# Out-projections, stores, loads and first products of a half at other places of a written-out order; the fill of a phase's middle score bank given to VectorE

## The reference, cut to what matters

```python
x = L0_attn_x                                  # (8, 1024, 256), float32
x = x + 0.5 * ffn(layernorm(x))                # 8 routed experts (top 2) and a shared one
x = x + attention(layernorm(x))
x = x + 0.5 * ffn(layernorm(x))

def attention(x):                              # x is (b, s, 256); 16 heads of 64
    h = layernorm(x) * ln_scale + ln_bias
    c_q, c_kv = h @ w_down_q.T, h @ w_down_kv.T            # 128 wide each
    q, k, v = c_q @ w_up_q.T, c_kv @ w_up_k.T, c_kv @ w_up_v.T
    q, k = rope(q), rope(k)
    attn = softmax(q @ k.T / 8)                # over 1024 keys
    return (attn @ v) @ w_out.T + x
```

## Time and profile before

| what | value |
|---|---|
| median of 3 runs | 4161.7 us |
| lowest and highest of them | 4150.89 and 4165.04 us |
| the profiled execution's own time | 4144.14 us |
| its span, first to last instruction | 4142.2 us |
| its mean granted TensorE clock | 0.986 |
| attention part, from its first transpose to the next part | 528 to 3630 us of the span |

### The profile page before, as it was taken

One profiled execution on the slowest core, in us unless ns is written; L12 is line 12 of the kernel. 1 busy time (PEld: TensorE's weight loads), 2 busy tenths in 40 slices (PEclk: granted clock), 3 DMA queues, 4 the chain that ended last, 5 costly groups with the idle time before them and its releaser, 6 DMA issues. The chain is left out here.

```text
span 4142.2 us, 65717 instructions
## 1 busy us (share of the span) xinstructions
PE 3935.1 (95%) x24908; PEld 2209.9 (53%) x24908; DVE 2790.7 (67%) x3709; ACT 2630.8 (64%) x3276; POOL 2955.7 (71%) x1634
## 2 busy tenths in 40 slices
PE   7999979999999999999999999999999999989999
PEld 6888834444444444444444444444444444468888
DVE  5665567777767776776777667767777777556563
ACT  4545447766766676667667766766676667645544
POOL 3444448878878887878788888878887888634443
PEclk9999989999999999999999999999999999989999
DMA  3333221112211211121122122111211121132331
GB/s 108 112 123 101 87 92 52 55 57 65 71 59 52 73 62 52 58 82 52 52 66 72 55 63 73 58 54 57 78 61 52 52 83 55 40 122 96 123 113 62
DMA packets 192771, 300.36 MB, mean 73 GB/s; under 512 B 50327, under 2 KB 100936, under 8 KB 191816
## 3 DMA queue, kind: packets, MB, share of 16 engines
q1 hardware_dynamic: 192456, 296.17, 22.3%
HBM read 201.20 MB, written 26.73 MB: 55 GB/s over the span
## 5 line engine op out<-in xcount | busy, mean ns | idle before, releaser
L1078 DVE TENSOR_REDUCE atNM<-atPS 128x2 f32<-128x1024 f32 x1024 | 1229.6, 1221 | 520.8 <-PE atPS L889 519.5
L1019 ACT ACTIVATE atPT<-atPS 128x1024 f32<-128x1024 f32 x1024 | 1036.1, 1020 | 581.6 <-PE atPS L910 573.4
L1177 POOL TENSOR_TENSOR atACC<-atACC,atPT 128x1024 f32<-128x1024 f32 x510 | 1243.7, 2439 | 85.6 <-ACT atPT L1019 35.5
L921 PE MATMUL atPO<-atPT,atV 128*64 128x512 f32 x4096 | 1030.5, 606 | 26.5 <-ACT atAT L1026 26.1
L1010 ACT ACTIVATE atPS<-atSH 128x1024 f32<-128x1024 f32 x768 | 779.0, 1024 | 182.9 <-DVE atNM L1078 149.7
L1177 POOL TENSOR_TENSOR atACC<-atPT 128x1024 f32<-128x1024 f32 x255 | 609.4, 2390 | 242.3 <-PE atOT L943 142.8
L921 PEld LDWEIGHTS atPO<-atPT,atV 128*64 128x64 f32 x4096 | 255.4, 137 | 478.4 <-issue 391.1
L910 PE MATMUL atPS<-atQH,atKL 64*128 64x512 f32 x2048 | 457.1, 443 | 46.1 <-ACT atPS L1010 35.2
L889 PE MATMUL atPS<-atKH,atQH 64*128 64x512 f32 x2048 | 456.4, 443 | 20.8 <-ACT atQH L999 15.3
L910 PE MATMUL atPS<-atQL,atKH 64*128 64x512 f32 x2048 | 405.8, 392 | 0.0
L910 PE MATMUL atPS<-atQH,atKH 64*128 64x512 f32 x2048 | 405.7, 392 | 0.0
(11 more groups left out here) (278 smaller groups left out, 6511.9 us busy)
## 6 DMA issues: line engine op xcount, KB each, us to landing
atSH<-atMD SPq DMA_DIRECT2D x128, 512.0 KB, 4.4
atVT<-atR SPq DMA_DIRECT2D x508, 128.0 KB, 2.1
f1GB<-f1GD SPq DMA_DIRECT2D x128, 256.0 KB, 6.9
f2GB<-f2GD SPq DMA_DIRECT2D x128, 256.0 KB, 6.9
atRSUM<-atRD SPq DMA_DIRECT2D x126, 256.0 KB, 4.0
X<-x SPq DMA_DIRECT2D x4, 1024.0 KB, 5.7
XS<-x SPq DMA_DIRECT2D x16, 256.0 KB, 3.8
x<-X SPq DMA_DIRECT2D x16, 256.0 KB, 3.0
```

The costliest lines, as they stand in the source:

```text
L921: ins = pe.eng.matmul(PO[HI[h], :], V[n % 2][:, j, HI[h]], PT[k % NPT][:, h, :], start=j == 0, stop=j == T - 1)
L1019: act.eng.activation(PT[k % NPT][:, :, :], PS[ring.of[step]][:, :, :], ACT.Exp, scale=SCALE).then_inc(grown.sem)
L1078: dve.eng.tensor_reduce(NM[:, q // 4, :, q % 4, t], PS[ring.of[step]][:, :, :], AX.X, ALU.max, negate=True).then_inc(most_out.sem)
L1177: pool.eng.tensor_tensor(total[:, :, :], begun[:, :, :], PT[k % NPT][:, :, :], ALU.add).then_inc(gathered.sem)
```

## The change

The order of the steps changes in five ways, and who fills in one:

- `stats` of the next batch go from periods -40.. to -35.., `spread` from -36 to -31, `norm` from -33.. to -29...
- The four `outward` steps of a pair of heads go from ticks 0, 1, 7, 9 (counted from period 24) to 1, 14, 15, 16.
- The four `store` steps go from periods 25, 26, 28, 30 to 27, 31, 32, 32, and each `load` stands four periods behind its store (before: three, three, two, two).
- Where a half ends at tick x of a phase (x % 8 == 7), `attend` of tile x + 1, the first of the next half, is held over to the next phase, behind its first other steps and ahead of its own first attend; in such a phase `attend` x now stands behind both fills and the other steps.
- `gather` steps follow their attends in the same way.
- `filler` now goes by the place in the phase: the fill of tile x + 2 (x a multiple of 3) is VectorE's, all others are ScalarE's. It was by j: tiles 3 and 7.

```diff
                     if b:
                         for i in range(4):
-                            at(end, m, -40 + i, ("stats", b, i))
+                            at(end, m, -35 + i, ("stats", b, i))
                         for k in range(T):
-                            at(end, m, -33 + k, ("norm", b, k))
-                        at(end, m, -36, ("spread", b))
+                            at(end, m, -29 + k, ("norm", b, k))
+                        at(end, m, -31, ("spread", b))
...
-                    for u, (period, table) in enumerate([(24, early), (24, late), (27, late), (28, late)]):
+                    for u, (period, table) in enumerate([(24, late), (31, early), (31, late), (32, early)]):
                         at(table, m, period, ("outward", m, u))
                 if p == NP - 1:
-                    for u, period in enumerate((25, 26, 28, 30)):
+                    for u, period in enumerate((27, 31, 32, 32)):
                         at(end, m, period, ("store", b, u))
                         if b + 2 < NB:
-                            at(end, m, period + 3 - u // 2, ("load", b + 2, u))
+                            at(end, m, period + 4, ("load", b + 2, u))
...
-            order = []
+            order, held = [], []
             for x in range(-42, 2 * PER * (NN + 4), 3):
                 order += tile("score", x) + most_of(x) + tile("fill", x + 2) + tile("score", x + 1)
-                order += others_of(x) + tile("attend", x - 1)
-                order += [step for step in tile("gather", x - 1) if step[3] % 4 and step[1:3] + (step[3] // 4,) != (NN - 1, 1, 1)]
+                order += others_of(x) + held + tile("attend", x - 1)
+                order += gathers(held + tile("attend", x - 1))
                 order += most_of(x + 1) + tile("score", x + 2) + most_of(x + 2)
-                if x % T == T - 1:
-                    order += tile("fill", x + 3) + tile("attend", x) + others_of(x + 1) + tile("fill", x + 4) + tile("attend", x + 1)
-                else:
-                    order += tile("fill", x + 3) + others_of(x + 1) + tile("fill", x + 4) + tile("attend", x) + tile("attend", x + 1)
-                order += [step for i in range(2) for step in tile("gather", x + i)
-                          if step[3] % 4 and step[1:3] + (step[3] // 4,) != (NN - 1, 1, 1)] + others_of(x + 2)
+                now, held = tile("attend", x), tile("attend", x + 1)
+                if x % T < T - 1:
+                    now, held = now + held, []
+                order += tile("fill", x + 3) + others_of(x + 1) + tile("fill", x + 4) + now + gathers(now) + others_of(x + 2)
...
-            def filler(j):
-
-                return 2 if j % 4 == 3 else j % 2
+            def filler(n, t, j):
+
+                x = (2 * n + t) * T + j
+                return 2 if x % 3 == 2 else x % 2
```

More of the change, by code:

```diff
@@ L711, in most_of, with gathers @@
                 return [("most", n, r // 2, r % 2)] if 0 <= n < NN else []
+            def gathers(attends):
+                return [("gather",) + s[1:] for s in attends if s[3] % 4 and s[1:3] + (s[3] // 4,) != (NN - 1, 1, 1)]
             def others_of(x):
                 return [step for (tick, _), table in (begin, early, late, end) if tick == x % 2 for step in table.pop(x, [])]
-            order = []
+            order, held = [], []
             for x in range(-42, 2 * PER * (NN + 4), 3):
                 order += tile("score", x) + most_of(x) + tile("fill", x + 2) + tile("score", x + 1)
-                order += others_of(x) + tile("attend", x - 1)
-                order += [step for step in tile("gather", x - 1) if step[3] % 4 and step[1:3] + (step[3] // 4,) != (NN - 1, 1, 1)]
+                order += others_of(x) + held + tile("attend", x - 1)
+                order += gathers(held + tile("attend", x - 1))
                 order += most_of(x + 1) + tile("score", x + 2) + most_of(x + 2)
-                if x % T == T - 1:
-                    order += tile("fill", x + 3) + tile("attend", x) + others_of(x + 1) + tile("fill", x + 4) + tile("attend", x + 1)
-                else:
-                    order += tile("fill", x + 3) + others_of(x + 1) + tile("fill", x + 4) + tile("attend", x) + tile("attend", x + 1)
-                order += [step for i in range(2) for step in tile("gather", x + i)
-                          if step[3] % 4 and step[1:3] + (step[3] // 4,) != (NN - 1, 1, 1)] + others_of(x + 2)
+                now, held = tile("attend", x), tile("attend", x + 1)
+                if x % T < T - 1:
+                    now, held = now + held, []
+                order += tile("fill", x + 3) + others_of(x + 1) + tile("fill", x + 4) + now + gathers(now) + others_of(x + 2)
             assert not any(table for _, table in (begin, early, late, end))
@@ L771, in attention @@
             shift = [sig(f"shift{t}", 16).expect(heads) for t in range(2)]
-            filled = [sig(f"filled{i}").expect([s for s in events("fill") if filler(s[2]) == i]) for i in range(3)]
+            filled = [sig(f"filled{i}").expect([s for s in events("fill") if filler(*s) == i]) for i in range(3)]
             score, grown = (sig(x).expect(events("score")) for x in ("score", "grown"))
@@ L901, in tensor @@
                         bank = PS[ring.of[step]]
-                        pe.wait_ge(*filled[filler(j)](n, t, j))
+                        pe.wait_ge(*filled[filler(n, t, j)](n, t, j))
                         pe.wait_ge(*high(n, 1))
@@ L1004, in scalar @@
                         act.eng.activation(ML[t][:, :], OT[0:8, 0:128], ACT.Copy).then_inc(row_out.sem)
-                    elif name == "fill" and filler(step[3]) < 2:
+                    elif name == "fill" and filler(*step[1:]) < 2:
                         _, n, t, j = step
@@ L1009, in scalar @@
                         act.wait_ge(*(grown if before[0] == "score" else most_out)(*before[1:]))
-                        act.eng.activation(PS[ring.of[("score", n, t, j)]][:, :, :], SH[t][:, :, :], ACT.Copy).then_inc(filled[filler(j)].sem)
+                        act.eng.activation(PS[ring.of[("score", n, t, j)]][:, :, :], SH[t][:, :, :], ACT.Copy).then_inc(filled[filler(n, t, j)].sem)
                     elif name == "score":
@@ L1078, in vector @@
                         dve.eng.tensor_reduce(NM[:, q // 4, :, q % 4, t], PS[ring.of[step]][:, :, :], AX.X, ALU.max, negate=True).then_inc(most_out.sem)
-                    elif name == "fill" and filler(step[3]) == 2:
+                    elif name == "fill" and filler(*step[1:]) == 2:
                         _, n, t, j = step
@@ L1211, in sync @@
                         for j in range(T - 3, T):
-                            sp.wait_ge(*filled[filler(j)].past(n - 1, t, j))
+                            sp.wait_ge(*filled[filler(n - 1, t, j)].past(n - 1, t, j))
                         sp.eng.dma_start(SH[t][:, :, :].rearrange("p h q -> p (h q)"),
```

## The result

| | before | after |
|---|---|---|
| median | 4157.92 us (4 runs) | 4110.51 us (4 runs) |
| lowest and highest | 4150.89, 4165.04 | 4105.59, 4111.56 |
| profiled execution | 4144.14 us | 4111.56 us |

The changed kernel takes 0.9884 of the time, 95% interval 0.9863 to 0.9904: 47 us less, where 15 were forecast, and 4110.5 lies just under the range's low end of 4112. Two differences must be kept apart. The medians are 47 us apart, the two profiled executions only 33.

A forecast was written before the change was run, and what follows sets the result against it. TensorE, busy 95% of the span, was taken as the bound, so only its waits count. Terms -17 - 11 + 6 + 22 - 14 + 6 - 7 = -15 us, from 4161.7 to 4147; range 4112 to 4176.

The forecast's parts named there:

- Held attend: At ends of halves, TensorE's wait for ScalarE's bank copy: 26 us removed, 9 returning at four places a round, 17 gained.
- Exponential and Q copy: ScalarE freed of a fill: exponentials start sooner, 11 us gained; next head's first maximum waits less for Q, 7 gained.
- Out-projections behind the division: First out-projection of a pair moves later and the norm's scales behind GpSimd's division: seven waits go, 14 us gained.
- VectorE's chain before the sum: In the phase making Q's low half, VectorE's fill lengthens its chain and delays the row sum: 22 us lost.
- Rival 1: Only the good parts show, VectorE's chain in the low-half phase having slack in most heads: -37 us, 4125; chance 0.24.
- Fill waits in general: VectorE's longer middle-bank fill loses 6 us; nine more lone attends between a phase's first two scores and maxima lose 6.
- Stores, loads, statistics, norms: Stores and loads keep their sizes, statistics and norms move before exponentials with room: nothing counted.
- From the profile to the median: Profiled execution, 4144.1 us, lay 17.6 below the median; the gain was taken from the median: 4161.7 - 15 = 4147.
- Rival 2: VectorE late in every rotary phase, its products delaying the bank's next user: 34 us, 4181, or 4164 with half; chance 0.17.
- rival 3: Waits only change name: score fills replace the half-turn wait, none of 17 us kept, +2, 4164; chance 0.16.
- rival 4: VectorE's added fills slow GpSimd's divisions and gathers by 36 us: 4183 if all reached TensorE; chance 0.03.

The follow-up runs named there:

- the hold alone: Kernel before with only the first attend of each half held over to the next phase: 4146.78 us, ratio 0.9985.
- The pairs: Kernel before with two parts of the change: new filler and held attend 4139.21 us, filler and new places 4143.30, held attend and places 4133.73.
- the scales alone: Statistics, spread and norm at their new periods, on the kernel before with new filler and held attend: 4124.72 us, ratio 0.9925 to the kernel before.
- the kernel that takes this fill back: Changed kernel with ScalarE filling the middle bank in the phase with Q's low half and the row sum (21 fills): 4092.00 us, ratio 0.9855.
- The filler alone: Kernel before with only the new choice of which engine fills: 4139.10 us, ratio 0.9966.
- the moved turns: Changed kernel with ScalarE filling in the low-half phase, and the second half's turns and latents two periods earlier: 4114.81 us, ratio 0.9904.
- the best one: Changed kernel with ScalarE filling in the low-half phase, and out-projections of each batch's second pair of heads at old places: 4075.62 us, ratio 0.9807.

## Why the prediction was wrong

The direction was right (faster had 0.50), the size not: -15 forecast, -47 measured. The working, term by term, against the start-to-start table:

- **Held attend: 17 forecast (26 less 9), 35 found.** This is the step that failed. "That leaves 0.2 to 0.4 us at each of four places a round" took it that the fills behind the held attend would become late. They do with the hold alone (fills 51.0), in phase 66 as long as the new places are missing (12.7 and 13.2), and in phases 42 and 90 with the new places but the old filler (6.7 and 9.3). In the changed kernel the scores at all four places are late by 4.3 us in all, less than the 9.7 before: the 9 us forecast as lost there were not lost. The prediction itself had the out-projections move "by 1, 13, 8 and 7 ticks" and did not ask in which phase they land: two of them in phase 63, as cover for that very fill. It priced the fills behind the held attend against the list with neither the new cover nor the fill that leaves ScalarE. And the 26 us of idle that the page shows were no upper bound: attends were late by 35, part of it matmuls at the lower clock behind such a wait (two of the five stretches of that profile follow the copy's). So half of the 18 us is the wait that did not come back, half the wait that was worth more than its idle time.
- **Exponential and Q copy: 18 forecast, 22 found.** Right. The Q-copy part (7 forecast) is 6: the maxima of phases 0 and 48 were late by 10.9 and are by 4.8. The pairs show that it depends on the filler (14.4 against 3.7 in phase 48).
- **Out-projections behind the division: 14 forecast, 16 found** and 0.39% from the scales alone. Right in size, but it was the scales' move that brought it.
- **VectorE's chain before the sum: +22 forecast, +13 found** start to start, +16.0 by the page. The mechanism is shown by the kernel that takes this fill back; the size was taken from a low half of 2.35 us, and low halves have a median of 2.12 before and 1.69 after, down to 1.2. Rival 1 (slack in other heads) was right in part.
- **Fill waits in general: 12 forecast (+6 for a longer fill, +6 for nine more lone attends), 17 found.** The direction is right; the scores' 17 also hold what came at the four places above, so that 21 were forecast for them in all. The filler alone, with the old places, already makes the scores 15 us later. The new places take the out-projection out of slot one in phases 48, 57 and 87 (22 us later there) and cover others, phase 0 above all (9.6 to 1.0), so that they add little in sum.
- **Stores, loads, statistics, norms: nothing forecast.** Left out was what out-projections at ticks 14 to 16 do to the turns beside them: +19, the rows of 16.7 us. The prediction looked at the queue of each engine and forgot the queue for bank OT. This error went against the gain: had it been counted, the forecast would have been further off. That the measured time lies only 1.5 us under the range is luck in this sense. With the 5 us of raise, value and row, these seven make -29 where the sum had -15.
- **From the profile to the median: 14 us.** "4161.7 - 15" takes the change as the same in every execution. But the profiled execution of before had 5 stretches of reduced clock and fewer late fills than another with 11 and 20 us more. A change that removes the waits that these stretches follow would take more from a usual execution than from a lucky one. How much of these 14 us the clock makes was not shown: six stretches of 1.5 us are 9, and the fills' waits differ as well (35.2 and 40.2).

The low end of the range was summed wrongly by 1: rival 1 with the two bounds is 4161.7 - 37 - 9 - 5 = 4111, not 4112; the measured 4110.5 lies under both.

Rival 2 did not come (no wait for a rotary product stands in front of an out-projection, and the one in front of rows fell from 1.6 to 0.2 us), rival 3 nearly holds for the hold alone, rival 4 is excluded by the gathers' mean.

Open: stores and loads were never tried apart from the out-projections, and why the moved turns cost 23 us where their waits grew by 19.1 was not followed further (its profile has stretches of reduced clock at 1970 to 1990 and 3110 us).

## What to carry to other kernels

In an order written out by hand the terms of a change do not add: work that is moved is cover that is moved. Before summing, write down for each bank handover which long step stands in front of it before and after the whole change, and price each wait against the new list; a wait removed by one edit is often kept from coming back only by another. And try to take back parts of a change that won: here one fill in three heads and one pair's out-projections, put back as they were, gave 35 us more (32 by ratios).

## What was not expected of the hardware

A wait of 1 to 2 us in a span in which TensorE is busy for 95% of the time can cost almost twice its length, since the matmuls behind it sometimes run at 1.2 GHz (3.58 us for 1.95, 3.39 for 1.94). It differs between executions of one program, and makes up part of their spread: the kernel before ranged over 4141.6 to 4170.6 us in all sessions, the changed one over 4105.6 to 4111.6, and the best one, whose profile has no such stretch, over 4072.5 to 4079.5.

The page's busy time of TensorE fell by 37 us for the same 24908 matmuls while the rest of its span grew by 5. Matmuls at the lower clock are counted as busy, and so, it seems, are short waits: of the 22 us that the maxima gained only 9 had been idle time. A forecast from idle rows alone can have even the sign wrong; start-to-start times of the same pair of steps nearly closed.
